# A token-embedding, attention and mixture-of-experts kernel: the second image block of a tile pair moved by a 101-column transpose, written ahead of the first

## What is computed

```
h  = layernorm_affine(concat(cls, patches @ W + b) + pos)      # 37 tokens
h  = concat(h, txt)                                            # 165 tokens x 256
h  = h + attn(layernorm(h))     # 16 heads of 16; each row keeps its 49 largest scores
h  = h + moe(layernorm(h))      # 64 experts, 8 per token, 128 places each, and a shared one
```

## Time and profile before

| | us |
|---|---|
| median of 3 runs | 3138.24 |
| lowest and highest | 3135.48, 3142.18 |
| profiled execution, first to last instruction | 3227.4 |
| its engines' busy time: PE, DVE, ACT, POOL | 2638.8, 2551.2, 2482.0, 2207.5 |

### The profile page before, as it was taken

The page is one execution under the profiler, slowest core; times in us unless marked ns, Lnnn a source line. Parts: engine busy times, 40 slices in busy tenths (PEclk is TensorE's granted clock), DMA queues, the critical chain, the costliest instruction groups (busy, mean ns, idle before and its releaser), DMA issues. The chain is left out here.

```text
span 3227.4 us, 81090 instructions
## 1 busy us (share of the span) xinstructions
PE 2638.8 (82%) x21777; PEld 2097.4 (65%) x21777; DVE 2551.2 (79%) x11421; ACT 2482.0 (77%) x11137; POOL 2207.5 (68%) x4328
## 2 busy tenths in 40 slices
PE   4688988988888888888888988888888888637774
PEld 3566766766666676666666766666766666437664
DVE  1798999989899899889899898988999888613221
ACT  2998988988888888889888898888989889301110
POOL 3467777777777777777777777777777777544554
PEclk8799999999999999999999999999999999858897
DMA  2001000001010000110000000101011000037774
GB/s 60 11 24 23 19 23 20 20 24 24 18 24 20 23 22 17 24 24 20 22 20 23 22 19 20 24 20 24 18 24 24 19 18 17 7 78 187 178 187 84
DMA packets 184206, 118.99 MB, mean 37 GB/s; under 512 B 100304, under 2 KB 175244, under 8 KB 183724
## 3 DMA queue, kind: packets, MB, share of 16 engines
q1 hardware_dynamic: 149356, 94.33, 10.6%
q0 software_dynamic: 34368, 19.34, 4.0%
HBM read 66.81 MB, written 33.40 MB: 31 GB/s over the span
## 5 line engine op out<-in xcount | busy, mean ns | idle before, releaser
L843 ACT ACTIVATE JK<-S,thr 128x165 f32<-128x165 f32 x2688 | 1120.5, 422 | 23.2 <-POOL thr L607 16.6
L664 POOL DMA_INDIRECT slot_token<-TOKI,SLOT x512 | 545.7, 1066 | 225.0 <-issue 193.7
L645 POOL TENSOR_SCALAR X<-S,nt 128x165 f32<-128x165 f32 x1344 | 590.4, 456 | 76.0 <-DVE LIST L1106 67.0
L831 ACT ACTIVATE E<-bank,nb 128x165 f32<-128x165 f32 x1344 | 517.0, 407 | 96.4 <-POOL cnt L627 78.6
L843 ACT ACTIVATION_READ_ACCUMULATOR JK<-S,thr 128x1 f32 x2688 | 512.3, 191 | 0.0
L1223 DVE SCALAR_TENSOR_TENSOR PR<-S,TV,E 128x165 f32<-128x165 f32 x1344 | 457.1, 395 | 0.0
L1031 DVE TENSOR_SCALAR_CACHE_REDUCE S<-bank 128x165 f32<-128x165 f32 x1344 | 361.5, 318 | 67.4 <-PE bank L1573 34.7
L1106 DVE MAX8 LIST<-X 128x8 f32<-128x165 f32 x1344 | 351.1, 316 | 5.4
L1589 PE MATMUL bank<-IDENT,PR 128*128 128x128 f32 x1344 | 224.3, 284 | 126.9 <-DVEq L1214 69.5
L1096 DVE TENSOR_TENSOR X<-X,flip 128x495 int32<-128x495 int32 x448 | 297.6, 665 | 0.0
L1593 PE MATMUL bank<-IDENT,PR 128*37 128x128 f32 x1408 | 293.3, 291 | 0.0
(11 more groups left out here) (201 smaller groups left out, 6633.1 us busy)
## 6 DMA issues: line engine op xcount, KB each, us to landing
S<-in_w_gate SPq DMA_DIRECT2D x64, 192.0 KB
S<-in_w_up SPq DMA_DIRECT2D x64, 192.0 KB
E<-in_w_down SPq DMA_DIRECT2D x64, 192.0 KB
x_rows<-X SPq DMA_DIRECT2D x64, 160.0 KB
H<-in_txt SPq DMA_DIRECT2D x64, 128.0 KB
QA<-QT SPq DMA_DIRECT2D x512, 10.3 KB
QB<-QT SPq DMA_DIRECT2D x512, 10.3 KB
out<-OT SPq DMA_DIRECT2D x64, 128.0 KB
```

The costliest lines, as they stand in the source:

```text
L645: last = pool.tensor_scalar(X[n % DEEP][:, t % GROUP, :], S[r % 2][:, t, :], nt[r % 2][:, t:t + 1], DOWN, ALU.add, ALU.mult)
L664: pool.indirect_dma_start(slot_token, bass.IndirectOffsetOnAxis(SLOT[r % 2][:, 0, k:k + 1], 0), TOKI[r % 2][:, :], None, bounds_check=SLOT ...
L831: act.activation(E[r % 2][:, t, :], chunks(bS[g % 3], GROUP, T)[:, t % GROUP, :], ACT.Exp, bias=nb[:, t:t + 1], scale=-1.0, accum_out=sz[: ...
L843: act.activation(JK[:, t % 4, :], S[r % 2][:, t, :], ACT.Sign, bias=(t0, t1)[n][:, t:t + 1], scale=-1.0, accum_out=(c0, c1)[n][:, t:t + 1] ...
```

## The change

In each pair but the first, the high tile's 37 image columns are no longer moved by a product with the identity. PR is read as one flat row per partition, and the 101 columns that end with the high tile's 37th (the last 64 columns of the tile before it, and its first 37) are transposed to partitions 0 to 100, so that the wanted 37 arrive at partitions 64 to 100. This is written ahead of the low tile's transpose, which then overwrites partitions 0 to 36. In the pair p = 0 the product stays, and is also written first.

```diff
             def transposes(i, n):
 
+                rows = PR[:, :, :].rearrange("p t n -> p (t n)")
                 if n == 0:
                     pe.wait_ge(s_sure, i + 1)
...
                 for p in range(2 * n, min(2 * n + 2, PAIRS)):
                     at = P * (p % 4)
-                    pe.transpose(bI[0:IMG, at:at + P], PR[:, p, 0:IMG], IDENT[:, :])
-                    last = pe.matmul(bI[UPPER:UPPER + IMG, at:at + P], PR[:, MIXED + p, 0:IMG], IDENT[:, :],
-                                     start=True, stop=True, skip_group_check=True)
+                    if p == 0:
+                        pe.matmul(bI[UPPER:UPPER + IMG, at:at + P], PR[:, MIXED, 0:IMG], IDENT[:, :],
+                                  start=True, stop=True, skip_group_check=True)
+                    else:
+
+                        hi = (MIXED + p) * T + IMG
+                        pe.transpose(bI[0:UPPER + IMG, at:at + P], rows[:, hi - UPPER - IMG:hi], IDENT[:, :])
+                    last = pe.transpose(bI[0:IMG, at:at + P], PR[:, p, 0:IMG], IDENT[:, :])
                 last.then_inc(s_tr, 1)
```

## The result

| | before | after |
|---|---|---|
| median, us | 3135.2 (6 runs, 3126.0 to 3142.2) | 3121.8 (6 runs, 3118.0 to 3125.9) |
| profiled execution, span | 3227.4 | 3122.5 |
| busy PE, DVE, ACT, POOL | 2638.8, 2551.2, 2482.0, 2207.5 | 2405.6, 2543.6, 2472.6, 2208.9 |

The ratio after to before is 0.9961 (95% interval 0.9944 to 0.9978): 0.4% faster, 13 us.

The account below looks back on a forecast made before the run. No single engine was taken as the bound, but a loop of DVE, ACT and PE. 7 + 6 + 16 - 8 = 21 and 5 more gave 26 us: 3138 - 26 = 3112 us, range 3045 to 3155, likeliest 3095 to 3128.

Parts of the forecast that it names:

- The step on PE: PE's transpose calls: two pairs take 0.55 us instead of 1.22, saving 3.35 us a sample, 214 us over 64.
- The rival that something else stops PE: PE's transpose calls: the product is not what stops PE; 2.1 us a sample saved, 3122 us; chance 0.08.
- 0.21 us a pair: Lower bound on PE: 37-column changes still stop 0.20 us, so a pair saves about 0.21, the sample 2.1 us.
- (a): Call 0, before back_xt: its 0.35 us counts in only 19 of 61 iterations, a gain of 7 us.
- (b): Call 5, before the context: ACT's wait of 6.3 us in 25 iterations goes, a gain of 6 us.
- the 5 us for call 0s at 1.2 GHz: Call 0 at 1.2 GHz, where work takes nearly twice as long: an estimated 5 us more gain.
- (c): Calls 1 to 4 bring front_qk and front_v forward; a fifth of ACT's 79.5 us waits at VZ and KT, 16 us.
- (d): At the context: PE idles more, so 4 more starts at 1.2 GHz are charged, a loss of 8 us.
- All hidden: Attention loop: DVE's own list binds in every iteration, PE's saving is idle time only; 3138 us, within 6; chance 0.15.
- The late releases are real in the runs: At KT and VZ: PE's lead covers late releases, 79.5 us come off ACT, 93 us in all; 3045 us; chance 0.20.
- Slower, by the clock: At the context and ahead of call 0: PE waits more, 13 iterations lose 3.6 us each; 3159 us; chance 0.17.
- VZ and KT "much more in the profile than in the runs": Sign at ACT's waits for front_v and front_qk: they should shrink much more in the profiled execution than in the runs.

Follow-up runs that it names:

- grouped: Kernel before with a call's low-tile transposes written first and the high tiles' products behind them; 3129.83 us, ratio 0.9972.
- second group: Follow-up runs on a chip of their own, where the unchanged kernel before took 3237.4 us in its median.
- before_again: The kernel before, unchanged, run once more for a second profile; 3132.93 us, profiled span 3131.2.
- first and third group: Follow-up runs on two other chips, where the unchanged kernel before took 3138.0 and 3134.0 us in its median.
- only_1_to_4_b: Changed kernel with the product put back in calls 0 and 5, the transpose staying in calls 1 to 4; 3122.6 us, ratio 0.9962.
- fill_ctx: Changed kernel with five useless products between transposes 5 and the context; 3139.45 us, ratio 1.0010 to the kernel before.
- before_fill_again: Kernel before with eight useless products, four ahead of the transposes of call 0 and four behind; 3131.0 us, ratio 0.9992.

## Why the prediction was right, and where it was not

**The step on PE was right.** 0.55 us a four-tile call; matmuls 21777 to 21137; no idle time ahead of L1599, and ahead of L1600 only behind the product that stays. The 3.35 us a sample take calls 0 and 5 from the forecast, since waits hide where these end. The rule drawn on for it (TensorEngine Tiling (Array Packing) in the Trainium skill, that a change of tiling mode drains the engine) agrees with grouped too: the change to the products and back once less, 0.25 us less. The rival that something else stops PE is out, though its 3122 us is the very number that was measured: that is chance. Its 0.21 us a pair don't follow from its own words either (a pass of 0.14 and a stop of 0.20 are 0.34).

**The sum was too large and its terms stood in the wrong places.** 26 us were forecast, 13 and 9 came. That the time fell into the likeliest stretch, 3095 to 3128, is in part luck: none of the four terms stands as it was written.

- *(a) and (b), 7 + 5 + 6 us for calls 0 and 5.* None of it shows. With calls 1 to 4 alone the time was 3122.6 us, with all calls 3125.3, and on the second group's chip calls 0 and 5 alone made the kernel 14 us slower. Of the 21 us that call 0 saves in 61 iterations 13 are spent waiting for X (63.6 us in before_again, 76.9 now). The 26.8 us of the earlier trace rows, on which 42 iterations were written off and 19 counted, belong to the other kind of chip. No run shows the 5 us for call 0s at 1.2 GHz.
- *(c), 16 us.* The waits at VZ and KT it was to shorten don't exist on the chips of the first and third group. The step that failed is the discount itself: I took the 89 us between the span and the median to mean that the late releases were a disturbance of one execution and present in part in the runs. The wait at VZ is in every profile of the second group, and neither is in any of the nine of the other kind. Yet calls 1 to 4 are enough for the gain, and the first 0.25 us of each are enough for it, as far as these intervals tell (grouped, where 0.25 us came off call 0 as well). Which wait gave it I can't name: DVE's sum of waits is the same before and after, and what fell is its busy time at L1063; its wait at HM fell from 13.0 to 5.7 and 9.8 us, ACT's at L869 from 9.4 to 0, but only_1_to_4_b has 15.3 us at L869 and is no slower.
- *(d), -8 us for the clock at the context.* The clock did fall there (320 to 374 ns a pass), and nobody waits for it (fill_ctx). At back_glu ACT does wait, but there the slow clock was in the kernel before as well, and the change altered it little: 330 ns a pass in before_again, 336 and 332 with the change.

**The rivals.** *All hidden* (3138) was half of the truth: of the 204 us that PE saves in 61 iterations, 153 turned into waits of its own (321 us of named waits in before_again, 474 in after) and 47 into slower sums (127.3 and 127.4 us busy there, 151.5 and 150.4 now). *The late releases are real in the runs* was half right on the chip of the second group: they are real, calls 1 to 4 are worth 34 us there, against 93 that I gave it with calls 0 and 5. Of the waits it was to cover only KT's go; VZ's grow. *Slower, by the clock* did not come. Two iterations of after (stretch, length, engines, PEclk), against the earlier trace rows:

```profile
1470.20:1510.30 40.10, 32.75 (x317) 28.57 (x318) 38.91 (x178) 37.77 (x172) 31.87 (x66) 0.99 0.07 20
1510.30:1553.70 43.40, 34.92 (x304) 30.17 (x304) 39.13 (x176) 38.51 (x175) 31.57 (x65) 0.89 0.12 26
```

The slow kind is still there, but no more often. Between two starts of L1228 the granted clock is below 0.93 in 22 of 63 iterations of before_again and in 21 of after. The rule cited beside it (TensorE: Matmul & The Clock Gate in the Trainium skill, Part 4, that transposes don't count as activity) would also have the clock fall, from 0.97 to 0.95 as measured; but PE's longer waits could do that as well. In grouped, where every product is still there and PE's waits are 369 us, the clock is 0.96 and a pass of the sums 349 ns, so at least a part comes without the rule.

**The signs.** VZ and KT "much more in the profile than in the runs" could not be tested as meant, for the two profiles are of different kinds of chip.

## What to carry to other kernels

A profiled span that lies some per cent from the median of the runs may be that of another chip, with waits that the others lack, and not the same schedule with a disturbance: profile the kernel again, and weigh only waits that both show, before anything is priced with them. Time freed on an engine that waits anyway is first of all room: here 3.35 us an iteration were worth 0.2 to 0.4%, and the same time partly filled with eight useless products, at the place where PE's idle time was followed by work that others wait for, 1%. Ask of a lost clock who waits for the slow stretch; the one where the change lost most (the context) was free.

## What the runs showed of the hardware that was not expected

- One program took 3134 and 3138 us on two chips and 3237 us (13 runs within 17 us) on a third. On the third, in the wait shown, ACT resumed 3.16 us after PE's last product that it needed, since the signal came late; on the others it does not wait there. DVE's wait for the rows that DMA loads (L1004, H) differs too: 27 to 31 us in the five profiles of the slower kind, 8 to 11 in the nine others. The same calls 1 to 4 were worth 34 us on the one kind and 11 on the other.
- Float32 transposes of 37, 101 and 128 columns follow one another 0.11 us apart in any mix; a plain product into partitions 64 to 100 starts 0.20 us behind a transpose, and putting two such products of a call side by side takes 0.25 us off the call.
- A higher granted clock is no gain by itself: the profiled execution of before_fill_again has 0.958 over the whole span and its runs a ratio of 0.9992, only_1_to_4_b 0.923 and 0.9962.
